# A pooling stage in which the 5/7 class reads its gathered source directly, and the next source gather waits for the first pooling pass

## The chip, the cores and the metric

One Trainium2 chip, one core of it. The time is the device time of the whole program in microseconds (us); the median of three runs before the change is 4460.77 us (4456.75 to 4460.80). The profile is of one further execution of the same program.

## What is computed

The input is 16 images of 512 channels, 64 x 64, float32. Two layers, each added to its own input:

```
x = x + relu(conv1x1(concat(gn(x), 25 neighbour correlations / norm)) + bias)      # layer 0
z = gn(x)                                                                          # layer 1
s = relu(w2 @ relu(w1 @ mean(z) + b1) + b2)          # one number per plane (image, channel)
q = clip(floor(s), 0, 5)
pools = maxpool_same(z, k) for k in (1, 3, 5, 7, 9, 11, 13)
x = x + (q + 1 - s) * pools[q] + (s - q) * pools[q + 1] + z
```

Each of the 8192 planes (16 images x 512 channels) thus needs two neighbouring pool sizes of its own: class q needs the windows 2q+1 and 2q+3. Class 2, the "third class" of this text, needs the 5 x 5 and the 7 x 7 maximum.

## The kernel before, in words

**First layer.** Up to about 2.6 ms the program goes through the images in chunks of eight rows. It writes the result y to DRAM (`y_planes`), and beside it `wide_planes`, in which each element is already the maximum of five neighbours in its row. Nothing of that is touched by the change.

**Sorting.** The classes are computed (`sort_planes`, L913), and the planes are sorted by class into tiles of 128 planes, one plane in a partition. A class fills whole tiles, so that NT is 72: in this data 67 tiles hold planes (classes 0 to 5 with 11, 11, 13, 11, 11 and 10 tiles, in this order: tiles 0 to 10, 11 to 21, 22 to 34, 35 to 45, 46 to 56, 57 to 66) and the last five are empty.

**Second layer, one tile t.** Five steps, each on its own engine, each engine with its own program of tiles. They meet by semaphores alone:

- POOL (GpSimd) gathers by indirect DMA: the records and the y planes of tile t into one of four buffers `bufs` (`gather`, L504), and the source planes of `wide_planes` into the single buffer `source` (`gather_source`, L521). For classes 0 and 1 the source gather has the indices of one plane only, all others being out of bounds, and the planes come from `bufs`; for class 2 and up it brings 128 planes of 16 KB.
- ACT (ScalarE) copies the source, or for classes 0 and 1 the y planes, into the single buffer `ypad` with four border columns left and right (`pad_plane`, L664: L673 the planes, L674 and L675 the borders).
- DVE (VectorE) takes maxima in two passes (`pools`, L1054; every operation is recorded as L1062). The first pass of class 2 goes over rows of `ypad` (`source_rows`, L1100), in 4 operations, and its second pass has 2 operations of 4096 elements. Classes 0 and 1 have 3 operations in the first pass. After the first pass `s_rows` is raised, after the second `s_pool`.
- PE (TensorE) sums the plane, the small and the large pool with diagonal matrices in eight PSUM banks (`mix`, L1383 and `mix_banks`, whose last product is L1406). It starts a bank when ACT has read it out for the tile before.
- ACT adds the constant and writes the banks back into `bufs` (`results`, L690; L695, eight times), then makes the diagonals of a later tile (L687). POOL scatters the tile to the output by indirect DMA (`scatter`, L535; L539).

**Order on the engines.** An engine takes its steps in the order in which they are written, so this order matters:

```
POOL  step t:  gather_source(t+1), wait for the write of t-2, gather(t+2), scatter(t-1)
ACT   step t:  pad_plane(t+1), results(t-1), diagonals(t+1)
DVE   tile t:  first pass, second pass
PE    tile t:  mix(t)
```

`scatter(t-1)` waits for `results(t-1)`; `gather_source(t+1)` is therefore behind `scatter(t-2)`. Before it issues, `gather_source(t)` waits until ACT has padded tile t-1 (`s_ypad`), since `source` may be overwritten then, copies the indices (L528) and issues (L531). `pad_plane(t)` waits until DVE has finished the first pass of t-1 (`s_rows`) and until the source has landed (`sourced`). DVE's tile t waits for its padding (`s_ypad`), for `mix(t-2)` (L1141 to L1143), and for its own last tile.

Of the kernel before, what the change touches and what calls it, by code (L numbers as in the profile page):

```python
# [15 lines left out]
P = 128  # L16
# [72 lines left out]
def build(nc, x, wt, wturn, bias, w1t, b1, w2t, b2, consts, out):  # L89
# [21 lines left out]
    with ctx:  # L111
# [108 lines left out]
        pos[0] = 0  # L220
        bufs = v(BUFS * PIX).rearrange("p (b n) -> p b n", b=BUFS)
        WP = W + 2 * PADC
        source = v(PIX)
        ypad_f = v((H + 2 * PADY) * WP)
        ypad = ypad_f.rearrange("p (h w) -> p h w", w=WP)
        hbuf_f = v((H + 2 * PADR) * W)
        hbuf = hbuf_f.rearrange("p (h w) -> p h w", w=W)
# [88 lines left out]

        GROUPED = 3 * QUADS * 16
        STATS_CHAIN = 7
        STATS_AT = 4

        def xs(ct, lo, n, par):
# [118 lines left out]
        def _(pool):  # L440
# [80 lines left out]
            def gather_source(t, b):  # L521

                if not (isinstance(t, int) and t == 0):
                    pool.wait_ge(s_ypad, t)
                    pool.sem_inc(s_issue, 1)
                    pool.wait_ge(sourced, t * 16)
                pool.sem_inc(s_issue, 1)
                pool.tensor_copy(src_idx[:, b:b + 1], src_ids[:, bass.ds(t, 1)]).then_inc(s_src, 1)  # L528
                pool.wait_ge(s_src, t + 1)
                pool.sem_inc(s_issue, 1)  # L530
                pool.indirect_dma_start(out=source, out_offset=None, in_=wide_dram[:, :],  # L531
                                        in_offset=bass.IndirectOffsetOnAxis(ap=src_idx[:, b:b + 1], axis=0),
                                        bounds_check=NPL - 1, oob_is_err=False).then_inc(sourced, 16)
# [43 lines left out]
        def _(act):  # L577
# [86 lines left out]
            def pad_plane(t, u):  # L664
                act.wait_ge(gathered[u], turns_done(t, u))
                if not (isinstance(t, int) and t == 0):
                    act.wait_ge(s_rows, t)
                act.wait_ge(sourced, (t + 1) * 16)
                with act.If(class_of(t) < NCLS):
                    at = act.value_load(src_at[0:1, bass.ds(t, 1)], min_val=0, max_val=BUFS)  # L670
                    rows_ = arena[:, bass.ds(at * PIX, PIX)].rearrange("p (h w) -> p h w", w=W)
                    inside = ypad[:, PADY:PADY + H, :]
                    act.activation(inside[:, :, PADC:PADC + W], rows_, ACT.Copy)  # L673
                    act.activation(inside[:, :, 0:PADC], rows_[:, :, 0:1].to_broadcast([P, H, PADC]), ACT.Copy)  # L674
                    act.activation(inside[:, :, PADC + W:WP], rows_[:, :, W - 1:W].to_broadcast([P, H, PADC]), ACT.Copy)\  # L675
                        .then_inc(s_ypad, 1)
                with act.Else():
                    if not (isinstance(t, int) and t == 0):
                        act.wait_ge(s_ypad, t)
                    act.sem_inc(s_ypad, 1)  # L680
# [55 lines left out]
        def _(dve):  # L736
# [176 lines left out]
            def sort_planes():  # L913
# [118 lines left out]
                link(dve.scalar_tensor_tensor(sel, tcls, float(NCLS), sel, ALU.is_lt, ALU.mult))  # L1032
                dve.tensor_scalar(not_first, ident[:, 0:1], -float(NPL), float(NPL), ALU.mult, ALU.add)
                link(dve.tensor_scalar(unsel, sel, -1.0, 1.0, ALU.mult, ALU.add))
                dve.tensor_copy(tmod, tmod_i)
                link(dve.tensor_scalar(unsel, unsel, not_first, None, ALU.mult))
                link(dve.tensor_scalar(src_f, tmod, -1.0, float(BUFS), ALU.mult, ALU.add))
                link(dve.tensor_tensor(src_f, src_f, sel, ALU.mult))
                link(dve.tensor_tensor(src_f, src_f, tmod, ALU.add))
                dve.tensor_copy(src_at, src_f)  # L1040
# [13 lines left out]
            def pools(t, s, k):  # L1054

                used = [0]

                def op(dst, a, b, wait=True, signal=s_own):

                    if wait and used[0]:  # L1060
                        dve.wait_ge(s_own, t * OWN + used[0])
                    ins = dve.tensor_tensor(dst, a, b, ALU.max)  # L1062
                    ins.then_inc(signal, 1)
                    if signal is s_own:
                        used[0] += 1

                def window(src, mid, dst, r, signal=s_own):

                    m, w = half_m, big[:, s, :]
                    op(mid(m, 0, 31 + r), src(1 - r, 31 + r), src(2 - r, 31 + r))  # L1070
                    core = m
                    if r in (2, 4):
                        op(mid(w, 0, 30 + r), mid(m, 0, 30 + r), mid(m, 1, 30 + r))
                        core = w
                    if r == 4:
                        op(mid(m, 0, 32), mid(w, 0, 32), mid(w, 2, 32))
                        core = m
                    if r in (3, 5):

                        op(mid(w, 0, 14 + (r + 1) // 2, 1), mid(m, 1, 14 + (r + 1) // 2, 2),  # L1080
                           mid(m, 2, 14 + (r + 1) // 2, 2))
                        if r == 5:
                            op(mid(w, 0, 16, 1), mid(w, 0, 16, 1), mid(w, 1, 16, 1))
                        op(mid(m, 0, 16, 2), mid(w, 0, 16, 1), mid(m, 0, 16, 2))
                        op(mid(m, 1, 16, 2), mid(w, 0, 16, 1), mid(m, r, 16, 2), wait=False)
                    op(dst(0), mid(core, 0, 32), src(-r, 32))
                    op(dst(1), mid(core, 0, 32), src(1 + r, 32), wait=False, signal=signal)

                planes = ypad[:, PADY:PADY + H, :]

                def cols(i, n):
                    return planes[:, :, PADC + i:PADC + i + 2 * n - 1:2]

                def cols_mid(a, i, n, step=1):
                    return a.rearrange("p (h w) -> p h w", w=36)[:, :, i:i + step * (n - 1) + 1:step]

                def rows(i, n):
                    return hbuf[:, PADR + i:PADR + i + 2 * n - 1:2, :]

                def source_rows(i, n):  # L1100
                    return ypad[:, PADY + i:PADY + i + 2 * n - 1:2, PADC:PADC + W]

                def rows_mid(a, i, n, step=1):
                    return a.rearrange("p (h w) -> p h w", w=W)[:, i:i + step * (n - 1) + 1:step, :]

                sm_, bg = small[:, s, :, :], big[:, s, :].rearrange("p (h w) -> p h w", w=W)
                inner = hbuf[:, PADR:PADR + H, :]
                small_rows = lambda e: sm_[:, e::2, 1:W + 1]

                def shifted(d):  # L1110
                    return planes[:, :, PADC + d:PADC + d + W]

                if k < 2:
                    window(cols, cols_mid, lambda e: inner[:, :, e::2], 1, signal=s_rows)
                elif k == 2:

                    window(source_rows, rows_mid, small_rows, k, signal=s_rows)
                elif k < 5:
                    op(inner, shifted(2 - k), shifted(k - 2), signal=s_rows)
                else:  # L1120
                    core = cols_mid(half_m, 0, 32)
                    op(core, cols(-2, 32), cols(3, 32))
                    op(inner[:, :, 0::2], core, cols(-3, 32))
                    op(inner[:, :, 1::2], core, cols(4, 32), wait=False, signal=s_rows)
                dve.wait_ge(s_rows, t + 1)
                if k == 0:

                    window(rows, rows_mid, lambda e: bg[:, e::2, :], 1, signal=s_pool)
                else:
                    if k != 2:  # L1130
                        window(rows, rows_mid, small_rows, k)
                    op(inner, sm_[:, :, 0:W], sm_[:, :, 2:W + 2])
                    op(bg, hbuf[:, PADR - 1:PADR - 1 + H, :], hbuf[:, PADR + 1:PADR + 1 + H, :], signal=s_pool)
                assert used[0] <= OWN
                dve.sem_inc(s_own, OWN - used[0])

            def tile(t, s):
                cls_t = dve.value_load(cls_i[0:1, bass.ds(t, 1)], min_val=0, max_val=NCLS)

                def waits():  # L1140
                    dve.wait_ge(s_ypad, t + 1)  # L1141
                    if not (isinstance(t, int) and t < 2):
                        dve.wait_ge(s_mix, (t - 1) * 8)  # L1143
                    if not (isinstance(t, int) and t == 0):
                        dve.wait_ge(s_pool, t)

                def branch(lo, hi):
                    if lo == hi:
                        waits()
                        if lo == NCLS:  # L1150
                            dve.sem_inc(s_own, OWN)
                            dve.sem_inc(s_rows, 1)
                            dve.sem_inc(s_pool, 1)
                        else:
                            pools(t, s, lo)
                        return
# [31 lines left out]
            for q in range(4):  # L1188
                dve.wait_ge(y_stored[q], 16 * B)
            for side in (slice(0, PADY), slice(PADY + H, H + 2 * PADY)):  # L1190
                dve.memset(ypad[:, side, :], LOWEST)
            for side in (slice(0, PADR), slice(PADR + H, H + 2 * PADR)):
                dve.memset(hbuf[:, side, :], LOWEST)
            dve.wait_ge(s_rec, 16)
# [242 lines left out]
```

## Time and profile before

| | |
|---|---|
| median of three runs | 4460.77 us |
| the profiled execution's own time | 4458.1 us |
| its span | 4456.4 us |
| PE busy | 3936.7 us, 88% |
| DVE busy | 3559.3 us, 80% |
| POOL busy | 2281.9 us, 51% |
| ACT busy | 1898.3 us, 43% |
| moved by DMA | 781.57 MB, 175 GB/s on average |

The span is the time from the first to the last instruction in the trace. Busy time of an engine is what its instructions took, not what they needed: an instruction that is held up while it runs counts as busy. The time of a whole engine says little here, because the program has a first layer, a sorting part and six stages of tiles with different limits. A row of the trace ends with the idle time of the engine just before it and with who ended it, in square brackets. On POOL and ACT that is often "issue", where the wait was for a DMA or lay in a branch, and the releaser isn't named.

### The profile page before, as it was taken

Reading aid. Unit: us, or ns where it says so; the run is one execution under the profiler, and the core shown is the slowest. Engines: PE = TensorE matmul, PEld = TensorE weight load, DVE = VectorE, ACT = ScalarE, POOL = GpSimd, SP = SyncE. Lnnn points to the kernel's source line nnn. Section 1 sums busy time; section 2 is a strip of 40 time slices with the busy share of each in tenths; the row PEclk is TensorE's granted clock in tenths of the full one; section 3 lists DMA queues with packets and bytes.
Section 4 is the critical chain, followed back from the end, with each engine's and each line's share of the span. In section 5 each row is a group of like instructions: output and inputs, shape, how many; then the busy total and the mean of one; then the engine's idle time right before and its main releaser. Section 6 shows DMA issues by size and latency. Waiting matters only on the chain. (4 is left out here: it accounts for less than half of the span.)

```text
span 4456.4 us, 76765 instructions
## 1 busy us (share of the span) xinstructions
PE 3936.7 (88%) x23656; PEld 2172.9 (49%) x23657; DVE 3559.3 (80%) x3528; ACT 1898.3 (43%) x2964; POOL 2281.9 (51%) x1793
## 2 busy tenths in 40 slices
PE   5999999999999999999999965789888888888885
PEld 3556555555555655656556642334333333333332
DVE  6887788787888788878878766689866799999993
ACT  3444444444444544444444513444333333333332
POOL 3555555555555555555555514355544444556442
PEclk9999999999999999999999977889998999999897
DMA  4444344544544444444443334444456566565551
GB/s 183 154 170 176 132 173 167 176 148 157 188 155 162 168 151 167 177 147 158 176 167 138 121 80 171 191 184 189 188 219 237 194 235 250 224 245 208 226 211 50
DMA packets 252266, 781.57 MB, mean 175 GB/s; under 512 B 98151, under 2 KB 98151, under 8 KB 229991
## 3 DMA queue, kind: packets, MB, share of 16 engines
q1 hardware_dynamic: 219600, 417.85, 26.8%
q0 software_dynamic: 32288, 358.95, 20.8%
q8 instruction: 206, 3.38, 0.3%
q14 instruction: 172, 1.40, 0.1%
HBM read 428.22 MB, written 409.08 MB: 188 GB/s over the span
## 5 line engine op out<-in xcount | busy, mean ns | idle before, releaser
L1062 DVE TENSOR_TENSOR arena<-arena 128x2048 f32<-128x2048 f32 (+5 forms) x539 | 1442.5, 2695 | 263.0 <-ACT arena L675 223.8
L1402 PE MATMUL psum<-arena 128*128 128x512 f32 x1072 | 606.7, 650 | 295.5 <-ACT arena L695 209.4
L1208 PE MATMUL psum<-arena 128*128 128x256 f16 (+1 forms) x6344 | 763.1, 276 | 47.2 <-DVE arena L808 34.4
L447 POOL TENSOR_TENSOR arena<-arena 128x512 f16<-128x512 f32 x512 | 721.5, 1417 | 146.5 <-ACT arena L597 140.6
L1231 PE MATMUL psum<-arena 128*128 128x512 f16 x2048 | 776.8, 379 | 0.0
L1233 PE MATMUL psum<-arena 128*128 128x512 f16 x2048 | 776.2, 379 | 0.0
L1232 PE MATMUL psum<-arena 128*128 128x512 f16 x2048 | 776.2, 379 | 0.0
L1208 PEld LDWEIGHTS psum<-arena 128*128 128x128 f16 x6344 | 610.9, 102 | 160.1 <-DVE arena L808 44.5
L673 ACT ACTIVATE arena<-arena 128x4096 f32 x67 | 242.5, 3619 | 1045.5 <-issue 1045.5
L456 POOL TENSOR_TENSOR arena<-arena 128x512 f32 (+1 forms) x512 | 635.1, 1273 | 10.7 <-ACT arena L611 6.7
L820 DVE BATCH_NORM_STATS2 bny<-arena 128x6 f32 (+1 forms) x512 | 355.6, 694 | 341.2 <-POOL arena L456 328.0
L1406 PE MATMUL psum<-arena 128*128 128x512 f32 x1072 | 579.2, 624 | 0.0
L611 ACT ACTIVATE arena<-psum,bias_sb 128x512 f32<-128x512 f32 x512 | 338.1, 686 | 541.8 <-POOL arena L456 339.8
L466 POOL CAST arena<-arena 128x128 f16<-128x128 f32 x128 | 37.3, 291 | 1006.1 <-DVE arena L852 1006.1
L1402 PEld LDWEIGHTS psum<-arena 128*128 128x128 f32 x1072 | 215.3, 207 | 591.5 <-issue 324.7
L1404 PE MATMUL psum<-arena 128*128 128x512 f32 x896 | 494.6, 635 | 0.0
L595 ACT ACTIVATE arena<-arena,gbias,grstd 128x512 f32 (+1 forms) x512 | 413.6, 808 | 48.9 <-POOL arena L447 46.0
L597 ACT ACTIVATE arena<-arena,gbias,grstd 128x512 f16 (+1 forms) x512 | 411.4, 803 | 0.0
L539 POOL DMA_INDIRECT out<-arena x67 | 120.0, 1791 | 551.7 <-issue 551.7
L1406 PEld LDWEIGHTS psum<-arena 128*128 128x128 f32 x1072 | 218.2, 204 | 288.1 <-issue 288.1
L808 DVE TENSOR_TENSOR arena<-psum,cst 128x256 f32<-128x256 f32 x496 | 287.4, 579 | 80.2 <-PE psum L1208 80.2
L695 ACT ACTIVATE arena<-psum,arena 128x512 f32<-128x512 f32 x536 | 319.5, 696 | 64.4 <-PE psum L1406 64.4
(161 smaller groups left out, 4328.5 us busy)
## 6 DMA issues: line engine op xcount, KB each, us to landing
arena<-in_x SPq DMA_DIRECT2D x64, 2048.0 KB, 13.3
wide_planes<-arena SPq DMA_DIRECT2D x128, 1024.0 KB, 5.3
y_planes<-arena SPq DMA_DIRECT2D x64, 2048.0 KB, 7.8
arena<-arena SPq DMA_DIRECT2D x1536, 8.0 KB, 1.8
arena<-wide_planes,arena POOLq DMA_INDIRECT x72
arena<-plane_records,arena POOLq DMA_INDIRECT x67
arena<-y_planes,arena POOLq DMA_INDIRECT x67
out<-arena POOLq DMA_INDIRECT x67, 7.9
```

The source lines that it names most:

```text
L447: pool.tensor_tensor(gl[:, ct, slot], g32[:, ct % 2, :], gh[:, ct, slot], ALU.subtract).then_inc(s_gl, 1)
L456: pool.tensor_tensor(y, y, relu[:, o % 2, :], ALU.add).then_inc(s_added, 1)
L595: act.activation(g32[:, ct % 2, :], piece, ACT.Identity, bias=gbias[:, ct:ct + 1], scale=grstd[:, ct:ct + 1])
L597: act.activation(gh[:, ct, (c % RING) * CW:(c % RING + 1) * CW], piece, ACT.Identity, bias=gbias[:, ct:ct + 1], scale=grstd[:, ct:ct + 1]) ...
L1062: ins = dve.tensor_tensor(dst, a, b, ALU.max)
L1208: return pe.matmul(dst, w, m, start=(k == 0), stop=(k == nk - 1))
L1231: pe.matmul(dst, h, gh[:, ct, slot], start=(ct == 0), stop=False)
L1232: pe.matmul(dst, h, gl[:, ct, slot], start=False, stop=False)
L1233: last = pe.matmul(dst, l, gh[:, ct, slot], start=False, stop=(ct == CT - 1))
L1402: pe.matmul(dst, diag[:, s, 0, :], bufs[:, u, b * CW:(b + 1) * CW], start=True, stop=False)
L1404: pe.matmul(dst, diag[:, s, 1, :], small[:, s, b * ROWS:(b + 1) * ROWS, 1:W + 1], start=False, stop=False)
L1406: pe.matmul(dst, diag[:, s, 2, :], big[:, s, b * CW:(b + 1) * CW], start=False, stop=True)\
```

## The change

The buffer `source` gets two rows above and two below it (`source_pad`), filled once with the lowest float; `ypad` loses its own. Class 2's first pass on DVE reads `source_pad` and waits for `sourced` instead of `s_ypad`. ACT's copy to `ypad` stays for all classes, class 2 among them. Since DVE may now be reading `source`, `gather_source(t)` waits for `s_rows` of tile t-1 beside `s_ypad`, for every class. The table that holds where each tile's planes come from is now in units of two rows (SRC_STEP).

```
-        source = v(PIX)
-        ypad_f = v((H + 2 * PADY) * WP)
+        source_pad = v((H + 2 * PADY) * W).rearrange("p (h w) -> p h w", w=W)
+        source = source_pad[:, PADY:PADY + H, :].rearrange("p h w -> p (h w)")
+        ypad_f = v(H * WP)
...
                 if not (isinstance(t, int) and t == 0):
                     pool.wait_ge(s_ypad, t)
+                    pool.sem_inc(s_issue, 1)
+                    pool.wait_ge(s_rows, t)
                     pool.sem_inc(s_issue, 1)
                     pool.wait_ge(sourced, t * 16)
...
-                    at = act.value_load(src_at[0:1, bass.ds(t, 1)], min_val=0, max_val=BUFS)
-                    rows_ = arena[:, bass.ds(at * PIX, PIX)].rearrange("p (h w) -> p h w", w=W)
-                    inside = ypad[:, PADY:PADY + H, :]
-                    act.activation(inside[:, :, PADC:PADC + W], rows_, ACT.Copy)
+                    at = act.value_load(src_at[0:1, bass.ds(t, 1)], min_val=0, max_val=SRC_AT)
+                    rows_ = arena[:, bass.ds(at * SRC_STEP, PIX)].rearrange("p (h w) -> p h w", w=W)
+                    act.activation(ypad[:, :, PADC:PADC + W], rows_, ACT.Copy)
...
-                dve.tensor_copy(tmod, tmod_i)
+                link(dve.tensor_copy(tmod, tmod_i))
                 link(dve.tensor_scalar(unsel, unsel, not_first, None, ALU.mult))
-                link(dve.tensor_scalar(src_f, tmod, -1.0, float(BUFS), ALU.mult, ALU.add))
+                link(dve.tensor_scalar(tmod, tmod, float(PIX // SRC_STEP), None, ALU.mult))
+                link(dve.tensor_scalar(src_f, tmod, -1.0, float(SRC_AT), ALU.mult, ALU.add))
...
                 def source_rows(i, n):
-                    return ypad[:, PADY + i:PADY + i + 2 * n - 1:2, PADC:PADC + W]
+                    return source_pad[:, PADY + i:PADY + i + 2 * n - 1:2, :]
...
-                def waits():
-                    dve.wait_ge(s_ypad, t + 1)
+                def waits(k):
+                    if k == 2:
+                        dve.wait_ge(sourced, (t + 1) * 16)
+                    else:
+                        dve.wait_ge(s_ypad, t + 1)
```

## Rows read from the trace of the kernel before

**Rows 1.** The page: the span.

```profile
span 4456.4 us, 76765 instructions
```

**Rows 2.** Busy us by stretch (PE, PEld, DVE, ACT, POOL), clock, DMA: classes 0, 1, 2, 5.

```profile
2700.00:2918.00 218.00, 158.79 (x320) 67.28 (x320) 149.67 (x66) 100.25 (x152) 89.59 (x75) 0.84 0.48 186
2918.00:3180.00 262.00, 237.18 (x512) 102.61 (x512) 247.09 (x89) 112.14 (x170) 149.53 (x77) 0.92 0.47 181
3180.00:3537.00 357.00, 297.36 (x624) 127.38 (x624) 233.65 (x78) 127.13 (x192) 172.66 (x91) 0.90 0.56 218
...
4109.00:4389.00 280.00, 228.93 (x480) 97.84 (x480) 275.65 (x120) 102.03 (x159) 109.79 (x72) 0.91 0.51 197
```

**Rows 3.** Waits, 3232 to 3537 us: who, for whom, total us, times, longest.

```profile
DVE arena L1062 <- ACT arena L675: 104.3, 11, 9.7
```

**Rows 4.** ACT's timeline, class 2: start us, us, what, count, idle before.

```profile
3255.68 3.62 ACT L673 ACTIVATE arena<-arena 128x4096 f32 x1 [17.77 <-issue]
...
3259.81 4.72 ACT L695 ACTIVATE arena<-psum,arena 128x512 f32<-128x512 f32 x8
...
3283.67 3.62 ACT L673 ACTIVATE arena<-arena 128x4096 f32 x1 [18.03 <-issue]
...
3532.89 3.62 ACT L673 ACTIVATE arena<-arena 128x4096 f32 x1 [17.64 <-issue]
```

**Rows 5.** POOL's timeline, class 2: scatter, index copy, source gather.

```profile
3266.18 1.87 POOL L539 DMA_INDIRECT out<-arena  x1 [11.55 <-issue]
3268.06 1.34 POOL L528 COPY arena<-arena 128x1 int32 x1
3270.31 4.57 POOL L531 DMA_INDIRECT arena<-wide_planes,arena  x1 [0.91 <-POOL arena L528]
```

**Rows 6.** DVE's timeline, class 2: tile 25.

```profile
3260.14 9.21 DVE L1062 TENSOR_TENSOR arena<-arena 128x2112 f32<-128x2112 f32 x4 [9.48 <-ACT arena L675]
3269.51 8.89 DVE L1062 TENSOR_TENSOR arena<-arena 128x4096 f32<-128x4096 f32 x2 [0.15 <-DVE arena L1062]
```

**Rows 7.** POOL's timeline, the first tiles.

```profile
2703.64 2.28 POOL L531 DMA_INDIRECT arena<-wide_planes,arena  x1 [0.90 <-POOL arena L528]
...
2715.03 2.35 POOL L531 DMA_INDIRECT arena<-wide_planes,arena  x1 [0.90 <-POOL arena L528]
...
2733.40 1.01 POOL L539 DMA_INDIRECT out<-arena  x1 [9.19 <-issue]
```

**Rows 8.** PE's timeline, class 2: first and last products of tile 24.

```profile
3260.53 2.08 PE L1402 MATMUL psum<-arena 128*128 128x512 f32 x2 [4.45 <-ACT arena L695]
...
3282.59 1.02 PE L1406 MATMUL psum<-arena 128*128 128x512 f32 x2
```

**Rows 9.** DVE's timeline, tiles 0 and 1.

```profile
2700.41 27.46 DVE L1062 TENSOR_TENSOR arena<-arena 128x2048 f32<-128x2048 f32 x12 [17.05 <-ACT arena L675]
```

**Rows 10.** ACT's timeline, padding of tiles 1, 2 and 3.

```profile
2709.42 3.62 ACT L673 ACTIVATE arena<-arena 128x4096 f32 x1 [8.07 <-issue]
...
2722.32 3.62 ACT L673 ACTIVATE arena<-arena 128x4096 f32 x1 [7.70 <-issue]
...
2742.57 3.62 ACT L673 ACTIVATE arena<-arena 128x4096 f32 x1 [9.65 <-issue]
```

**Rows 11.** POOL's timeline, class 1 to 2: source gathers 22, 23, scatter 20.

```profile
3162.47 2.19 POOL L531 DMA_INDIRECT arena<-wide_planes,arena  x1 [0.91 <-POOL arena L528]
...
3184.41 1.02 POOL L539 DMA_INDIRECT out<-arena  x1 [8.38 <-issue]
...
3187.68 2.19 POOL L531 DMA_INDIRECT arena<-wide_planes,arena  x1 [0.91 <-POOL arena L528]
```

**Rows 12.** DVE's timeline, class 1 to 2: from tile 21's second pass.

```profile
3163.88 34.08 DVE L1062 TENSOR_TENSOR arena<-arena 128x2048 f32<-128x2048 f32 x11 [0.16 <-DVE arena L1062]
```

**Rows 13.** DVE's timeline, class 5: tile 59's last operation, then tile 60.

```profile
4188.51 37.07 DVE L1062 TENSOR_TENSOR arena<-arena 128x4096 f32<-128x4096 f32 x15
```

**Rows 14.** ACT's timeline, class 5: padding of tile 61.

```profile
4207.59 3.62 ACT L673 ACTIVATE arena<-arena 128x4096 f32 x1 [15.90 <-issue]
```

More of the change, by code:

```diff
@@ L318, in build @@
         STATS_CHAIN = 7
+        SRC_STEP = PADY * W
+        SRC_AT = BUFS * PIX // SRC_STEP + 1
         STATS_AT = 4
@@ L669, in pad_plane @@
                 with act.If(class_of(t) < NCLS):
-                    at = act.value_load(src_at[0:1, bass.ds(t, 1)], min_val=0, max_val=BUFS)
-                    rows_ = arena[:, bass.ds(at * PIX, PIX)].rearrange("p (h w) -> p h w", w=W)
-                    inside = ypad[:, PADY:PADY + H, :]
-                    act.activation(inside[:, :, PADC:PADC + W], rows_, ACT.Copy)
-                    act.activation(inside[:, :, 0:PADC], rows_[:, :, 0:1].to_broadcast([P, H, PADC]), ACT.Copy)
-                    act.activation(inside[:, :, PADC + W:WP], rows_[:, :, W - 1:W].to_broadcast([P, H, PADC]), ACT.Copy)\
+                    at = act.value_load(src_at[0:1, bass.ds(t, 1)], min_val=0, max_val=SRC_AT)
+                    rows_ = arena[:, bass.ds(at * SRC_STEP, PIX)].rearrange("p (h w) -> p h w", w=W)
+                    act.activation(ypad[:, :, PADC:PADC + W], rows_, ACT.Copy)
+                    act.activation(ypad[:, :, 0:PADC], rows_[:, :, 0:1].to_broadcast([P, H, PADC]), ACT.Copy)
+                    act.activation(ypad[:, :, PADC + W:WP], rows_[:, :, W - 1:W].to_broadcast([P, H, PADC]), ACT.Copy)\
                         .then_inc(s_ypad, 1)
@@ L1087, in window @@
                     op(dst(1), mid(core, 0, 32), src(1 + r, 32), wait=False, signal=signal)
-                planes = ypad[:, PADY:PADY + H, :]
                 def cols(i, n):
-                    return planes[:, :, PADC + i:PADC + i + 2 * n - 1:2]
+                    return ypad[:, :, PADC + i:PADC + i + 2 * n - 1:2]
                 def cols_mid(a, i, n, step=1):
@@ L1110, in shifted @@
                 def shifted(d):
-                    return planes[:, :, PADC + d:PADC + d + W]
+                    return ypad[:, :, PADC + d:PADC + d + W]
                 if k < 2:
@@ L1148, in branch @@
                     if lo == hi:
-                        waits()
+                        waits(lo)
                         if lo == NCLS:
@@ L1190, in _ @@
             for side in (slice(0, PADY), slice(PADY + H, H + 2 * PADY)):
-                dve.memset(ypad[:, side, :], LOWEST)
+                dve.memset(source_pad[:, side, :], LOWEST)
             for side in (slice(0, PADR), slice(PADR + H, H + 2 * PADR)):
```

## The prediction

> **What bounds the kernel now.** I read the views in this order. The page gives the span, 4456.4 us [rows 1], and no more that helps: the change lies behind 2.7 ms. Busy time by stretch shows what each class is limited by. DVE is busy 276 of 280 us in class 5 and 247 of 262 in class 1, but only 150 of 218 in class 0 and 234 of 357 in class 2 [rows 2]. So in class 2, where the change is made, neither DVE nor PE (297 of 357) is full. The waits say that DVE stands 104.3 us there for ACT's padding, 9.5 us a tile [rows 3]. That looks like the thing to remove. The timelines tell otherwise. ACT pads tile 25 at 3255.68 for 4.25 us, writes the results of tile 23 from 3259.81 for 4.72, and pads tile 26 at 3283.67 [rows 4]. POOL begins the scatter of tile 23 at 3266.18, 1.65 us after those results; the index copy and the source gather of tile 26 stand behind it, and the gather's issue ends at 3274.88 [rows 5]; 8.8 us later the padding begins (8.4 to 8.8 in the tiles of class 2; I take 8.55). That is a closed ring: **pad, results, scatter, index copy, source gather, landing, pad**, 27.7 us a tile (from 3255.68 to 3532.89 in ten tiles [rows 4]). DVE is not a link of it. It only waits for it. Classes 0, 3 and 4 are on the same ring; classes 1 and 5 hang on DVE and PE.
>
> DVE does enter in another way. POOL's copy ends at 3269.40, as DVE's first pass does (3260.14 + 9.21 = 3269.35 [rows 6]), and the gather, 1.01 us for such an instruction when DVE rests [rows 7], takes 4.57 and ends 0.9 us after the first 4096 operation (3269.51 + 4.43 = 3273.94) [rows 5, 6]. So **a POOL instruction that falls into a DVE maximum ends when that maximum ends, a DMA one 0.93 us later**. The Trainium skill, "SBUF — State Buffer", section "Who interferes with whom", says that a VectorE instruction with two SBUF inputs contends with a GpSimd one that reads SBUF; by that the trace agrees.
>
> **The change, part by part.**
>
> *DVE's class 2 tiles start earlier, by up to 5.7 us.* They no longer wait for the 4.25 us of padding, nor for the at most 1.5 us in which ACT reads its two numbers. DVE is not in the ring, so the gain is 0 by itself. ACT still pads, so its link stays. What is late next is mix(t-2), which DVE waits for too: mix(24) goes from 3260.53 to 3283.61 [rows 8], when tile 26's padding begins [rows 4]. So DVE starts not 5.7 but some 4.5 us earlier.
>
> *Term 1, the added wait in class 0: +14.5 us.* In the ring of class 0 the source gather comes behind a scatter, and the first pass is over by then. In the first three tiles there is no scatter ahead yet. source(1) was released at 2700.4 by padding 0; now it waits for the end of DVE's third operation, 2700.41 + 3 x 2.29 = 2707.2 (12 operations in 27.46 [rows 9]). Copy, held until the fourth ends, 2709.6; 0.9 to the issue, 2710.5, held to 2711.9, end 2712.8, where it was 2705.92 [rows 7]. From there to the padding 3.5 us as before: 2716.3 for 2709.42 [rows 10], DVE's tile 1 at 2720.6. source(2): 2720.6 + 6.8 = 2727.4; by the same steps the issue ends at 2733.0 for 2717.38, and padding 2 begins at 2736.5 to 2737.9 for 2722.32 [rows 7, 10] (3.5 us as for tile 1, 4.9 as for tile 2), +14.2 to +15.6. The results of tile 0 stand behind it on ACT: 4.25 + 4.7 later, 2745.4 to 2746.8. Before, PE ended them at about 2731.8, and the scatter began at 2733.40; now at about 2747.7, +14.3. With that scatter the ring begins to turn, source(3) is behind it and waits for nothing else, padding 3 moves from 2742.57 [rows 10] by as much. The ring has no slack through class 0, and class 1 begins when it delivers: I take **+14.5**. Bounds: +12, if the landing is quicker; +17, if one more POOL instruction falls behind a maximum.
>
> In class 1 the gate puts off POOL by up to 5 us a tile. The source's issue ends 12.3 us after DVE's start (6.8 gate, 9.1 copy, 11.4 + 0.93); with 3.5 or 4.9 to the padding and 4.25 for it, 20 to 21.5 us, and DVE takes 22.5 a tile (247 us for eleven [rows 2]): hidden, with 1 to 3 us to spare. If that cover went, each of 11 tiles would cost what is over.
>
> *Term 2, into class 2: +7.* source(22) is the first full gather. DVE's tile 21 ends its first pass at 3163.7 [rows 12]; the copy is held to 3166.1, the issue to 3168.4 + 0.93 = 3169.3, for 3164.66 [rows 11]. Padding 22 is 3.9 us later, with it scatter(20): 3188.3 for 3184.41 [rows 11]. There DVE is in tile 22 (start 3179.7, unchanged: three operations to 3186.7, the fourth to 3188.9, 4096s to 3193.5 and 3197.9). Scatter ends at 3189.9, the copy at 3193.5, the gather at 3198.9 for 3189.87 [rows 11], and 8.55 us later is padding 23, 8.4 us later than before. Tile 24 by the same steps: the gap is 7.0. Bounds +3.7 (only the gate of tile 22 counts) and +9.
>
> *Term 3, class 2 itself: +8.* Let DVE start tile t at D. Its fifth operation is over at D + 13.8, its sixth at D + 18.25. The scatter, about 10.5 us after the padding begins, now falls into the fifth, so that it ends at D + 14.7; the copy falls into the sixth; the gather comes at D + 19.2, when DVE rests, and ends at D + 20.2; padding t+1 is 8.55 behind: **D + 28.8**. D itself is the end of mix(t-2), 27.9 us after padding t-1 began (3283.61 - 3255.68), plus 0.2. Two tiles thus take 28.8 + 28.1 = 56.9 us, for 2 x 27.7 = 55.4 now: +0.75 a tile, eleven tiles, +8. Bounds: DVE starts as soon as the source lands, 27.3 a tile, -4; mix ends later than I take it, +1.2 a tile, +13. I take the middle, since mix's end has a row.
>
> *No cost.* Classes 3 and 4: the first pass is one operation of 4.43 us, over before the scatter, and the ring has the same steps as now. Class 5: DVE starts tile 60 at 4188.51 + 4.43 = 4192.9 [rows 13]; gate +6.8, issue's end +11.8, padding at 20 to 21, done at 25, DVE's next tile at 28.0; before, padding 61 began at 4207.59 [rows 14], 14.7 after that start. Hidden behind DVE with 3 us over; without that cover it would be a us or two in ten tiles. Two more semaphore instructions on POOL a tile run while the scatter issues. One dependent step more in the sorting, well under 1 us. Copies from `source_pad` are of equal size.
>
> **Sum.** 14.5 + 7 + 8 = +29.5 on the profiled execution's 4458.1 gives 4487.6. The median of the runs is 2.7 above that execution, so I forecast **4490 us**.
>
> **The rivals.**
>
> *The gate alone counts (4475 to 4480).* Term 1 and 3.7 to 4 us at tile 22, and in class 2 the holds of POOL come out even, as at the lower bound of term 3. For it: only the order of some 2 us steps decides. Against: rows 5 and 6 show the hold in both kinds of POOL instruction.
>
> *POOL's DMA instructions are not held at all, only its copies (4465).* Then in class 2 the scatter is done inside the fifth operation, the copy ends with it at D + 13.8, the gather at D + 15.8, padding follows at D + 24.3. Two tiles take 52.4 us, 1.5 a tile less than now, -17: 4460.8 + 14.5 + 7 - 17 = 4465. Against: the gather's 4.57 us beside 1.01 [rows 5, 7].
> A remark in the same section of the Trainium skill's "SBUF — State Buffer" has it that two-input maxima did not stall a DMA's issue; this would be its outcome.
>
> *The late start is swallowed (4461 to 4466).* DVE idles 7 to 8 us a tile in class 0, and a ring that ran ahead at the start might have lost its lead anyway. Against: padding 1 to 3 are links of the ring, and nothing later in class 0 is ahead of it.
>
> *Faster: DVE is the link in class 2 after all (4401).* If what POOL waits for were released by DVE, the 5.7 us would come off each of 13 tiles, -74, and with term 1 that is 4461 - 74 + 14.5 = 4401. For it are rows 3. It decides from the point at which pool(t-1), not the banks, holds PE back. Against: PE's first product waits for L695, that is for a bank [rows 8].
>
> *Worse (over 4504).* Cover in class 1 or 5 fails, or class 3 loses a us a tile like class 2: 4501 to 4511.
>
> **How the numbers follow.** My forecast 0.63, gate alone 0.17, swallowed 0.08, DMAs not held 0.02, faster 0.05, worse 0.05. My forecast's own range is, with the terms' bounds not all at one end, 4477 to 4503. The range that leaves out about 2 in 10 takes in the gate alone: **4474 to 4504**. A measurement of this kernel can tell 0.2%, 8.9 us: faster by more than that 0.05, within it 0.10, slower 0.85.
>
> **What would show it.** In the new profile: padding 3 (L673, copy to `ypad`) some 14 us later than 2742.57, and the same 14 at the start of class 1; POOL's copy and gather of the first tiles ended behind the third maximum; in class 2 DVE ended by PE's last product or a DMA instead of ACT, the copy grown from 1.34 to 3 or more us and the gather's issue shrunk from 4.57 to about 1; paddings 28 to 29 us apart for 27.7; classes 3 to 5 as long as now. I am wrong if the paddings in class 2 are 27.7 or less apart, or if the first tiles keep their times.

## The result, and the profile after

| | before | after |
|---|---|---|
| median, 4 runs each | 4458.76 us (4455.32 to 4460.80) | 4488.01 us (4484.72 to 4488.70) |
| ratio after to before, 95% interval | | 1.0067 (1.0055 to 1.0079) |
| the profiled execution's own time | 4458.1 us | 4484.7 us |
| its span | 4456.4 us | 4483.0 us |

The change costs 29 us, 0.67%. The page's first lines, the span and the engines' busy time, do not say where:

```profile
span 4483.0 us, 76901 instructions
PE 3932.8 (88%) x23656; PEld 2171.5 (48%) x23657; DVE 3559.3 (79%) x3529; ACT 1895.7 (42%) x2964; POOL 2243.9 (50%) x1793
```

DVE does the same 3559.3 us of work. Busy time by stretch, classes 0, 1, 2 and 5, in the columns of [rows 2]:

```profile
2703.00:2935.00 232.00, 161.55 (x320) 68.17 (x320) 149.33 (x66) 99.95 (x151) 86.58 (x75) 0.83 0.45 174
2935.00:3188.00 253.00, 227.84 (x512) 98.20 (x512) 246.02 (x88) 106.17 (x164) 158.20 (x77) 0.97 0.46 183
3188.00:3560.00 372.00, 301.40 (x625) 128.80 (x624) 234.58 (x79) 129.91 (x196) 142.40 (x92) 0.89 0.54 213
4134.00:4415.00 281.00, 228.14 (x480) 97.63 (x480) 276.03 (x121) 101.27 (x160) 97.12 (x72) 0.90 0.50 196
```

Class 0 is 14 us longer (232 for 218), class 2 15 (372 for 357), and class 1 is 9 us **shorter** (253 for 262), at a granted clock of 0.97 for 0.92. The stages cut by the starts of DVE's tiles in the two traces, in us:

| | before | after | difference |
|---|---|---|---|
| DVE starts tile 0 at | 2700.4 | 2703.4 | +3.0 |
| tile 0 to 3 | 46.6 | 60.9 | +14.3 |
| 3 to 11, the rest of class 0 | 171.3 | 171.2 | -0.1 |
| 11 to 22, class 1 | 261.4 | 253.2 | -8.2 |
| 22 to 24 | 52.7 | 56.5 | +3.8 |
| 24 to 35, class 2 | 305.0 | 317.7 | +12.7 |
| 35 to 57, classes 3 and 4 | 571.5 | 571.5 | 0.0 |
| 57 to the end of 66, class 5 | 280.0 | 280.5 | +0.5 |
| from there to the end | 67.5 | 68.1 | +0.6 |

The sum is +26.6, the difference of the spans. Tile 0's start lay between 2698.1 and 2706.1 in the kernels run here and 0.4 to 3.6 us apart in two executions of one program, so its +3.0 is not put down to the change. The medians lie 29.3 us apart, 2.6 more than the two profiled executions (4484.7 - 4458.1): after's is 3.3 us above its profiled execution, before's 0.7. A fourth run of the kernel before, 4455.32, has moved its median from 4460.77 to 4458.76.

**The first tiles.** ACT's timeline, paddings 1 to 3 and the results of tile 0 (cf. [rows 10]):

```profile
2719.19 3.62 ACT L677 ACTIVATE arena<-arena 128x4096 f32 x1 [14.81 <-issue]
...
2739.18 3.62 ACT L677 ACTIVATE arena<-arena 128x4096 f32 x1 [14.79 <-issue]
...
2743.31 4.72 ACT L699 ACTIVATE arena<-psum,arena 128x512 f32<-128x512 f32 x8
...
2759.88 3.62 ACT L677 ACTIVATE arena<-arena 128x4096 f32 x1 [10.74 <-issue]
```

POOL's timeline there (L533 is the index copy, L536 the source gather, L544 the scatter; cf. [rows 7]):

```profile
2710.52 2.10 POOL L533 COPY arena<-arena 128x1 int32<-128x1 int32 x1 [14.21 <-DVE arena L1067]
2713.52 2.29 POOL L536 DMA_INDIRECT arena<-wide_planes,arena  x1 [0.89 <-POOL arena L533]
...
2749.62 1.74 POOL L544 DMA_INDIRECT out<-arena  x1 [8.61 <-issue]
2751.38 1.58 POOL L533 COPY arena<-arena 128x1 int32<-128x1 int32 x1
```

DVE's tile 0 starts at 2703.43. The copy is released by DVE and ends at 2712.6, 9.2 after that start, as its fourth operation does; the gather's issue ends at 2715.8, 12.4 after (the prediction had 12.4). From the start of tile 0, paddings 1, 2 and 3 lie 6.7, 13.8 and 14.3 us later than before.

**Class 2.** Who kept DVE waiting there (cf. [rows 3], 104.3 us for ACT):

```profile
DVE arena L1067 <- PE psum L1412: 113.3, 11, 11.7
```

ACT is gone from the list, and DVE waits 9 us longer for PE in its place. DVE, ACT and POOL around tiles 25 and 26:

```profile
3272.85 9.21 DVE L1067 TENSOR_TENSOR arena<-arena 128x2112 f32<-128x2112 f32 x4 [9.42 <-PE psum L1412]
3282.21 8.88 DVE L1067 TENSOR_TENSOR arena<-arena 128x4096 f32<-128x4096 f32 x2 [0.15 <-DVE arena L1067]
3302.83 2.36 DVE L1067 TENSOR_TENSOR arena<-arena 128x2112 f32<-128x2112 f32 x1 [11.73 <-PE psum L1412]
```

```profile
3274.05 3.62 ACT L677 ACTIVATE arena<-arena 128x4096 f32 x1 [19.41 <-issue]
...
3301.83 3.62 ACT L677 ACTIVATE arena<-arena 128x4096 f32 x1 [17.82 <-issue]
```

```profile
3284.55 2.98 POOL L544 DMA_INDIRECT out<-arena  x1 [14.28 <-issue]
3287.55 3.59 POOL L533 COPY arena<-arena 128x1 int32 x1
3292.05 1.06 POOL L536 DMA_INDIRECT arena<-wide_planes,arena  x1 [0.91 <-POOL arena L533]
```

The steps of term 3 stand here: the scatter ends 0.9 us after DVE's fifth operation (3287.53, 3286.64), the copy with its sixth (3291.1), the gather takes 1.06 us where it took 4.57 [rows 5], and it ends at D + 20.3 (D is where DVE's tile starts, 3272.85). The padding comes 8.7 us behind.

**The hold, counted.** In the trace of the kernel before, from tile 0 to the end of tile 66, 219 of POOL's indirect DMAs are issued while a maximum runs: 218 of them end 0.83 to 1.0 us after the end of that same maximum. Of 126 index copies that begin in a maximum, 115 end with it; the other 11 end some 0.1 us after it. POOL's memset in front of one of these copies, which reads nothing, isn't held (count, then shortest, median and longest in ns):

```profile
L506 POOL MEMSET arena<- x72: 102/102/126, 2682.1 to 4429.7; 128x4 f32 x72
L507 POOL COPY arena<-arena x72: 180/1712/4386, 2682.1 to 4429.7; 128x1 int32 x64, 128x1 int32<-128x1 int32 x8
```

### The profile page after: what moved, and what is told of

Read it like the earlier page. It is cut to its first block and busy times, and to the rows that moved or that the text cites. A ratio compares the mean times of both kernels' runs of the same rounds, so it can differ in the third digit from the quotient of the medians.

```text
span 4483.0 us, 76901 instructions
## 1 busy us (share of the span) xinstructions
PE 3932.8 (88%) x23656; PEld 2171.5 (48%) x23657; DVE 3559.3 (79%) x3529; ACT 1895.7 (42%) x2964; POOL 2243.9 (50%) x1793
## 5 line engine op out<-in xcount | busy, mean ns | idle before, releaser
L544 POOL DMA_INDIRECT out<-arena x67 | 146.2, 2181 | 595.9 <-issue 595.9
L699 ACT ACTIVATE arena<-psum,arena 128x512 f32<-128x512 f32 x536 | 317.1, 697 | 39.6 <-PE psum L1412 26.1
```

## The experiments

Eleven runs follow, of eight new kernels and three repeats, in three groups (e1 to e4, e5 to e8, e9 to e11); each ratio is to the kernel before as it ran in the same group, with medians of 4462.75, 4462.07 and 4458.70 us. e3, e4, e6, e7 and e11 were measured once each and have no interval. All stage times are of one profiled execution.

### Pulling the change apart: the gate alone

`e1_gate_only` keeps everything of the change but DVE's new wait:

```
-                    if k == 2:
-                        dve.wait_ge(sourced, (t + 1) * 16)
-                    else:
-                        dve.wait_ge(s_ypad, t + 1)
+                    dve.wait_ge(s_ypad, t + 1)
```

> The change with one part undone: DVE's class 2 tiles wait for the padding again, all else stays, the gate on the first pass in every class too. If class 2 is slower because DVE starts early and so lies across POOL's scatter and index copy (my theory), the paddings of class 2 are 27.7 us apart as before, against 28.5 in the change; the first tiles stay 14 us late; the step from class 1 to 2 costs 4 us; median about 4460 + 14 + 4, less the 8 us that class 1 gained, 4470. The rival, that the gate itself slows class 2, expects 28.5 us here too and about 4485.

Measured: 4535.67 us (4532.55 to 4540.13), ratio 1.0161 (1.0143 to 1.0179), far above what every theory had. `e11_gate_only_again` is the same program, measured once:

> The change with DVE waiting for the padding in class 2, once more, one look. If class 1 has two patterns between which an execution falls by the clock's phase, its eleven tiles take either 253 or 261 to 264 us here (264 the first time); if the program decides, 264 again. Class 2 again 32.3 us a tile: the gate opens at the end of the first pass, just when the first 4096 operation begins, and holds copy and gather one operation each longer.

Measured: 4542.19; class 1 takes 264.3 us, for 264.2 in e1. In both, class 2 takes 32.3 us a tile (tiles 24 to 35: 354.8 and 354.7 us, for 305.0). POOL and DVE around tile 25 of the first:

```profile
3302.14 1.86 POOL L544 DMA_INDIRECT out<-arena  x1 [14.97 <-issue]
3305.76 4.17 POOL L533 COPY arena<-arena 128x1 int32 x1 [1.76 <-DVE arena L1067]
3310.84 4.44 POOL L536 DMA_INDIRECT arena<-wide_planes,arena  x1 [0.91 <-DMA out<-arena]
```

```profile
3296.10 9.21 DVE L1067 TENSOR_TENSOR arena<-arena 128x2112 f32<-128x2112 f32 x4 [14.01 <-ACT arena L679]
3305.47 8.89 DVE L1067 TENSOR_TENSOR arena<-arena 128x4096 f32<-128x4096 f32 x2 [0.15 <-DVE arena L1067]
```

The first pass ends at 3305.31. Before, the copy had slipped in 1.3 us ahead of that end and was over with it, and only the gather was held, by the fifth operation [rows 5, 6]. Now the gate opens at that end, 0.16 us before the fifth operation starts; that one holds the copy to 3309.9, and the sixth holds the gather to 3315.3. The gather ends 23.6 us after the padding's start (3291.64) where it was 19.2, and a tile takes **4.5 us more, one whole maximum**, for a wait that by itself is over 1.8 us after the scatter. So in class 2 (tiles 22 to 35) the gate costs 62 us (12.4 + 49.8), and the early start of DVE gives back 46 of them (8.6 + 37.1). What that start would be worth without the gate, nothing by the prediction, no run shows. "The gate costs little and DVE's start nothing", from which I had built my expectation, was wrong twice.

### The gate in class 2 only, and both kernels again

`e2_gate_class2_only` lets POOL wait for `s_rows` only where tile t-1 is of class 2:

```
+                    last = class_of(t - 1)
+                    with pool.If(last < 3):
+                        with pool.If(last < 2):
+                            pool.sem_inc(s_issue, 1)
+                        with pool.Else():
+                            pool.wait_ge(s_rows, t)
+                            pool.sem_inc(s_issue, 1)
+                    with pool.Else():
+                        pool.sem_inc(s_issue, 1)
                     pool.wait_ge(s_ypad, t)
                     pool.sem_inc(s_issue, 1)
-                    pool.wait_ge(s_rows, t)
-                    pool.sem_inc(s_issue, 1)
```

> The change, but POOL waits for the first pass only when the tile before is of class 2 (which is all that needs it). My theory: padding 3 at its old distance from the stage's start (the 14 us of the first tiles gone), class 2 at 28.5 us a tile as in the change. On class 1, where the change gained 8 us that I had not foreseen: if the gate's delays spread PE's work and so keep its clock up, class 1 is here as long as before (about 262 us for its tiles) and the median about 4475; if the gain came by the chance of the clock's phase at the stage's entry, class 1 may be of either length, and the median 4467 to 4475.

Measured: 4474.42 (4468.73 to 4485.01), ratio 1.0029 (1.0014 to 1.0043). Paddings 0 to 3 in ACT's timeline (L684 in this kernel) are back at the old distances; padding 1 is 9.1 us after DVE's start of tile 0, for 9.0 in the kernel before and 15.8 in the change:

```profile
2697.12 3.62 ACT L684 ACTIVATE arena<-arena 128x4096 f32 x1 [64.26 <-issue]
2710.50 3.62 ACT L684 ACTIVATE arena<-arena 128x4096 f32 x1 [8.19 <-issue]
2723.29 3.62 ACT L684 ACTIVATE arena<-arena 128x4096 f32 x1 [7.58 <-issue]
2743.89 3.62 ACT L684 ACTIVATE arena<-arena 128x4096 f32 x1 [10.12 <-issue]
```

Tile 0 to 3 takes 47.0 us, so term 1 is the gate. Class 2 is 56.5 + 317.7, as in the change. Class 1 takes 253.4 in the profiled execution (4469.52), the change's short time, with no gate in it.

`e3_after_again` and `e4_before_again` are the two kernels once more, measured once each:

> The change once more, one look. If the spacing by the gate makes class 1 shorter, it is 8 us shorter here too, with TensorE's clock at 2.4 GHz through most of it; if that was chance, it may be as before.

> The kernel before once more, one look. If its class 1 is a stable pattern, every second tile of class 1 again waits 2.3 us for PE and the granted clock falls to 1.2 GHz once in two tiles; if it was chance, some tiles have no such wait.

Measured: 4486.29 and 4457.85, class 1 253.3 and 261.6 us. In e4 DVE again waits five times, 2.3 us each, and the clock falls once in two tiles. So before, the change and the gate alone (e1, e11) each have the same class 1 in both of their profiles. That makes an accident of one execution unlikely and doesn't exclude it: class 1 isn't known for the runs without a profile, and they spread over more than its 8 us, from 4468.73 to 4485.01 in e2 and from 4446.54 to 4470.58 in the kernel before in that group.

### The index copy taken out of the ring

The copy L528 needs nothing that it waits for; it can be made a step earlier, in `gather`, behind the other index copy. `e5_before_copy_ahead` does so in the kernel before, `e6_after_copy_ahead` in the changed one:

```
                 pool.tensor_copy(idx[:, b:b + 1], ids_i[:, bass.ds(t, 1)]).then_inc(s_idx, 1)
+                pool.tensor_copy(src_idx[:, b:b + 1], src_ids[:, bass.ds(t, 1)]).then_inc(s_src, 1)
...
-                pool.tensor_copy(src_idx[:, b:b + 1], src_ids[:, bass.ds(t, 1)]).then_inc(s_src, 1)
                 pool.wait_ge(s_src, t + 1)
```

> The kernel before, with one instruction moved: POOL copies the indices of the source gather with those of the plane gather, two tiles ahead, not between scatter and source gather. My theory (a POOL instruction that falls into a DVE maximum is held until it ends): in class 2 the source gather then comes before the first 4096 operation and is held only by the fourth of the first pass, so that it ends 4.5 us earlier in each tile's ring; class 2 falls from 27.7 to 23.5 us a tile, class 0 by 1 or 2 us a tile, classes 3 and 4 by no more than DVE's wait of 0.9 to 1.8 us; median about 4390. The rival, that POOL's instructions merely take long, expects the copy's own 1.3 us a tile off and no more: class 2 26.4, median about 4430.

> The same move in the changed kernel. By the hold theory the gather is now held by DVE's sixth operation in class 2 as the copy was, and only 1 us a tile is gained there: 27.5 us for 28.9; class 0 as in the run before it; about 4460. The rival (the copy's own time, 3.5 us a tile in class 2) expects 25.4 us a tile there and 4440.

Measured: e5 4424.58 (4422.96 to 4425.30), ratio 0.9915 (0.9898 to 0.9931); e6 4457.77, a single run. e5 around a tile of class 2:

```profile
3234.53 1.88 POOL L539 DMA_INDIRECT out<-arena  x1 [9.39 <-issue]
3236.71 1.90 POOL L531 DMA_INDIRECT arena<-wide_planes,arena  x1 [0.30 <-issue]
```

```profile
3228.49 18.24 DVE L1062 TENSOR_TENSOR arena<-arena 128x2112 f32<-128x2112 f32 x6 [5.57 <-ACT arena L675]
```

The gather falls into the fourth maximum, which ends at 3237.7, and is over 0.9 us later, at 3238.6; 14.6 us after the padding began for 19.2 before. The hold theory gave just that for the issue, where the rival had 1.3 us. But a tile takes 25.7 us, not 4.5 less than 27.7: the source lands 9.7 us after the issue's end (3248.3), where it took 7.1 in e1 and in e9. So the total missed the theory's 4390 by 35 us, and stands nearer to the rival's 4430; it is the rows that decide between the two. The DMA view of 3225 to 3260 us (the last number is the time from issue to landing):

```profile
out<-arena POOLq DMA_INDIRECT x1, 8.9
arena<-wide_planes,arena POOLq DMA_INDIRECT x1, 11.6
```

The gather now follows the scatter by 2.2 us, and both move 2 MB. Of the 4.6 us won at the issue, 2.0 are left at the tile. In class 0, where the source gather brings one plane only, it lands 0.2 to 0.7 us behind the scatter (2783.80 and 2783.61 us in one tile), so that there the earlier issue brings nothing: class 0 is as long as before. The Trainium skill, "DMA: Bandwidth & Descriptors", section "Two DMAs through the same engine are not ordered", says that descriptors within one queue of one DMA engine start in order but are pipelined. The landings here fit that; no row shows the descriptors' own order.

In e6, class 2 takes 27.2 us a tile, within 0.3 of what was expected, where the rival had 25.4. Its total of 4457.77 for 4460 is in part luck: class 1 is back at 261.7 us (+8.5), against tiles 0 to 3 with 56.5 us for 60.9 and class 4 with 6.5 us less.

### Is ACT's dead copy a link?

In class 2 nobody reads `ypad` any more. `e7_no_padding_class2` skips that copy in the changed kernel and only counts `s_ypad` up; it was measured once:

```
+                cls_t = class_of(t)
+                with act.If(cls_t < 3):
+                    with act.If(cls_t < 2):
+                        copy_plane(t)
+                    with act.Else():
+                        if not (isinstance(t, int) and t == 0):
+                            act.wait_ge(s_ypad, t)
+                        act.sem_inc(s_ypad, 1)
```

> The change, but ACT leaves out the copy to ypad in class 2, which nothing reads any more. If the padding is a link of the ring, as I hold, the results come 4.25 us earlier and class 2 shortens, by what the holds leave of it: the scatter falls behind the fourth operation, copy and gather behind the fifth and sixth, some 26.5 us a tile for 28.9, 4460. If the padding is off the path that sets the pace (rival), class 2 stays at 28.9 and the time at 4487.

Measured: 4461.98; tiles 24 to 35 in 298.0 us, 27.1 a tile, or 26.5 without the last step into class 3 (32.4 us), and tiles 22 to 24 in 53.6. DVE's tile 26:

```profile
3294.56 7.01 DVE L1079 TENSOR_TENSOR arena<-arena 128x2112 f32<-128x2112 f32 x3 [8.34 <-DMA arena<-wide_planes,arena]
```

It starts when the source lands. The 4.25 us of a copy that nobody reads stood ahead of the results on ACT and so in the ring. Without it tiles 22 to 35 take 22.7 us less than in the change (351.5 for 374.2), and the one run is about as long as the kernel before in its group (4462.07).

### PE's products before the pools

PE waits for pool(t) before it starts, though its first product of each bank needs only the plane. `e9_products_ahead` is the changed kernel with these eight products issued first, and the wait behind them:

```
-                pe.wait_ge(s_pool, t + 1)
...
+                    pe.matmul(psum[:, b, :], diag[:, s, 0, :], bufs[:, u, b * CW:(b + 1) * CW], start=True, stop=False)
+                pe.wait_ge(s_pool, t + 1)
+                for b in range(8):
                     dst = psum[:, b, :]
-                    pe.matmul(dst, diag[:, s, 0, :], bufs[:, u, b * CW:(b + 1) * CW], start=True, stop=False)
```

> The change, and PE does the eight products that need no pool (plane times diagonal) before it waits for the pools, the other two of each bank after. mix then ends some 6 us sooner after a pool. My theory: in class 1 DVE never waits for mix(t-2) and its eleven tiles take 250 us, whatever the clock does; in class 2 DVE starts when the source lands, the pair of tiles 56.9 us long becomes 2 x 27.5, 14 us less in the stage; the last tile ends 6 us sooner. Median about 4465. The rival, that class 2's 28.9 us do not hang on mix(t-2), expects class 2 unchanged and 4479; that the clock sets class 1 in another way than by DVE's wait, 253 to 262 us there.

Measured: 4468.50 (4463.44 to 4471.31), ratio to before 1.0021 (1.0012 to 1.0031), 19.5 us below the changed kernel's median, which is of another group of runs. Class 1 takes 250.3 us and DVE waits for no mix there. Class 2 was to lose 14 us and took 317.8, as without the edit, which is what the rival expected. Its waits in class 2:

```profile
DVE arena L1067 <- PE psum L1414: 113.7, 11, 11.9
```

and PE's eight early products of tile 24 (L1407):

```profile
3271.58 10.20 PE L1407 MATMUL psum<-arena 128*128 128x512 f32 x16 [6.27 <-ACT arena L699]
```

PE starts when ACT frees the banks (L699), not when the pool comes, so all 24 products still lie behind that release and mix(24) ends where it did: 3295.5, and DVE's tile 26 starts at 3295.6, 2.6 us after its source landed. This supports term 3's reading that D is mix(t-2)'s end: the rival was right in the number and wrong in the cause. The spans of the two profiled executions (4465.3, 4483.0) differ by 17.7 us: 3.7 in tile 0's start, 2.9 in class 1, and 10.6 behind DVE's last operation (57.5 us for 68.1), where eight products of 0.86 us of the last mix are done before, and where in the changed kernel PE rested 4.3 us ahead of the last mix and its first three products took 1.9 to 2.1 us each for 1.02.

### The combinations

`e8_all_three`: the gate in class 2 only, no copy to `ypad` in class 2, the index copy ahead. `e10_all_and_products`: the same and PE's products first.

> The change with the gate in class 2 only, no padding in class 2, and the indices copied ahead. Start of the stage as before (14 us less than the change), class 2 limited by the sum of PE's eight banks and DVE, 23.4 us a tile, class 0 and 4 1 us a tile less: about 4385, faster than both kernels by 1.6% or more. If PE's clock or the DMAs set the pace of class 2 instead, 25 us a tile and 4405.

> The best version so far (gate in class 2 only, no padding there, indices copied ahead) with PE's eight products ahead of the pools. Class 1 250 us for 262, class 2 22.5 us a tile for 24.3, the end 6 us sooner: about 4376. If class 2 is by now limited by POOL's holds alone, 24 us a tile and 4393.

Measured: e8 4412.11 (4411.10 to 4414.34), ratio 0.9887 (0.9871 to 0.9904), class 2 24.3 us a tile; e10 **4391.93** (4386.24 to 4393.53), ratio 0.9850 (0.9834 to 0.9867), class 2 23.9 a tile, class 1 250.3. e10 missed 22.5 us a tile and 4376 and came out at the alternative, 24 us and 4393; that POOL's holds are what limits it isn't shown, since DVE still waits mostly for PE. DVE's waits of e10 in class 2:

```profile
DVE arena L1086 <- PE psum L1433: 51.6, 9, 7.1
DVE arena L1086 <- DMA arena<-wide_planes,arena: 10.9, 3, 3.7
```

e10 is 1.5% quicker than the kernel before. With the held copy out of the ring, reading the source directly and leaving out the dead copy together do pay: e8 is 12 us below e5 (4412.11, 4424.58), which has the copy ahead alone, and its tiles 24 to 35 take 267.3 us for 282.8. e8 missed its expectation by 27 us: 10 in class 2 (24.3 a tile for 23.4), class 0 gained nothing from the copy ahead (its source lands behind the scatter's transfer), and class 1 fell back to 261.9.

## Why the prediction was right, and where it was not

**Term 1, +14.5: measured +14.3**, and gone where the gate is gone (e2). The ring that "has no slack through class 0" passed it on: tiles 3 to 11 take 171.2 us for 171.3, and the rival in which the late start is swallowed is refuted.

**Terms 2 and 3, +7 and +8, together +15: measured +16.5** between tiles 22 and 35. Cut by the paddings, as the prediction has them, both stand alone: against DVE's start of tile 22, paddings 22, 23 and 24 lie 4.2, 8.7 and 7.7 us later than before (forecast 3.9, 8.4 and 7.0), and the eleven tiles from padding 24 to 35 take 313.7 us for 304.9, +8.8. The table's 3.8 and 12.7 are the same sum cut by DVE's starts, which class 2 moves ahead and class 3, waiting for the padding again, moves back. The padding is 28.5 us apart (3244.67 to 3558.4 in eleven tiles) for the 28.45 forecast, and two tiles take 57.2 (3244.67 to 3301.83) for 56.9. The rival in which POOL's DMA instructions are not held, 4465, is refuted: the scatter takes 2.98 us and ends 0.9 after the maximum it fell into. So is the rival in which DVE is the link: its wait changed hands at once, and the time rose. One reading behind the hold was wrong and did no harm: the 1.01 us of [rows 7] isn't an instruction beside a resting DVE. That scatter begins 0.1 us before the end of the first maximum of tile 2 (2731.23 to 2733.52) and ends 0.9 us after it, as held ones do. The figure at rest is the change's 1.06 us.

**What the prediction did not have: class 1, -8.2.** I wrote that the gate is hidden there and the class keeps its length. The gate is hidden; the length is not fixed. Before, DVE waits for mix there:

```profile
DVE arena L1062 <- PE psum L1406: 11.3, 5, 2.3
```

Five times 2.3 us. PE, before, around one of these (clock below, by windows), and after at the same tile:

```profile
3080.81 1.02 PE L1406 MATMUL psum<-arena 128*128 128x512 f32 x2
3085.39 2.07 PE L1402 MATMUL psum<-arena 128*128 128x512 f32 x2 [3.56 <-issue]
3087.26 1.91 PE L1404 MATMUL psum<-arena 128*128 128x512 f32 x2
```

```profile
3075.01 1.12 PE L1408 MATMUL psum<-arena 128*128 128x512 f32 x2 [1.89 <-ACT arena L699]
```

Busy time and granted clock (before's row, then after's) for 3084 to 3092 us:

```profile
3084.00:3092.00 8.00, 6.61 (x9) 2.86 (x10) 7.79 (x5) 0.00 (x0) 6.68 (x3) 0.57 0.88 371
```

```profile
3084.00:3092.00 8.00, 8.00 (x20) 3.57 (x19) 7.95 (x3) 2.19 (x1) 5.93 (x4) 1.00 0.20 82
```

Before, from mix(13) on, PE rests 3.6 us ahead of every second mix, the granted clock is then at 1.2 GHz (0.5) for 6.8 us, and three products take 1.9 to 2.1 us each for 1.02. That mix ends 2.3 us after DVE could start, DVE waits, the next mix follows without a rest, and then PE rests 3.6 us again: once in 47.8 us, four times, behind a first rest of 7.3 us. After, PE rests 3.6 us ahead of mix(13) and then 1.9 us ahead of each of five mixes, the clock stays at 2.4 GHz from 2964 to 3121, and DVE waits for mix only twice, 3.0 us in all. In no profile does one pattern turn into the other within the class. The class took 261 to 262 us in the first (before twice, e5, e6, e8, and e1 and e11 with 264, 3.0 of which are DVE's wait for the padding of tile 22) and 253 to 254 in the second (after twice, e2, e7). The runs show that neither the gate (e1 has it and takes 264, e2 has none there and takes 253) nor class 2's part of the change (e6 has it and takes 261.7) decides it alone, and that it came out alike in both profiles of three programs; the clock falls or does not fall at tile 13 behind a rest of the same 3.6 us. What tips it there stays **open**; DVE's wait for mix(11) ahead of it is 2.0 to 2.4 us in the first pattern and 1.0 to 1.95 in the second, which goes with it and may not be the cause. An untested rival is chance, by the moment at which the clock changes against the tiles: the fall around DVE's start of tile 11 begins 0.9 to 1.7 us ahead of that start in the seven profiles of the first pattern, and in the four of the second 2.0 or 0.2 us ahead of it, or 1.2 and 1.5 behind it. What removes it is shown: with PE's products ahead, e10 has 250.3 us where e8 has 261.9.

**The sum.** +29.5 was forecast on the profiled time, and +26.6 measured: +14.3 + 16.5 - 8.2 in class 1, + 3.0 at tile 0's start, and +1.0 over the rest. The median, 4488.01 for 4490, is nearer than the sum deserves, and that is luck: against class 1's -8.2, which was left out, stand the +3.0 and +1.0, 1.3 us more in the three terms, and an after whose median happens to lie 3.3 us above its profiled execution.

**The rival "the gate alone counts" was badly priced.** It put the change at 4475 to 4480 and DVE's early start at nothing. The gate alone, e1, has 4536. The step that failed is "in class 2 the holds of POOL come out even": before, the copy has a lead of 1.3 us on the next maximum, and the gate takes it away; the rival's price left that out. That the full change came out at the forecast is due to D's shift: DVE is further on when POOL comes, so that the scatter and the copy fall into its last two maxima and the gather comes when DVE rests.

**My expectation for e9** failed for the reason that the prediction itself had named against DVE as the link: in class 2 PE's first product waits for a bank, not for a pool [rows 8].

## What to carry to other kernels

Find the ring of waits and price an edit by its links; a long wait of an engine (104 us of DVE here) may hang on the ring without being in it, and work left in the ring that nobody reads (ACT's copy) undoes the gain of a shortcut around it. A new wait costs not what it lasts but what it makes the waiting engine miss: here 1.8 us of waiting put POOL's copy behind one more maximum, 4.5 us a tile. Keep small POOL instructions out of a ring that DVE's two-input operations run beside, and issue work that needs no late input ahead of the wait for it.

## What the runs showed of the hardware

- **POOL is held to the end of a running maximum**, in every kernel here: the copy (0.18 us when DVE rests, 3.6 to 4.2 under a 4096 operation) ends with it, an indirect DMA's issue (1.0 us at rest, up to 5.2) 0.9 us after, while a memset (0.10 us) is not held. The Trainium skill, "SBUF — State Buffer", "Who interferes with whom", has the contention of a two-input VectorE instruction with GpSimd's reads, and the copy agrees with it; its remark that such operations did not stall a DMA's issue does not hold for these indirect ones (4.44 us in e1 for 1.06 in the change).
- **A 2 MB gather issued 2.2 us behind a 2 MB scatter lands 2.6 us later after its issue** (9.7 us in e5 for 7.1 in e1 and e9), so that 4.6 us won at the issue were 2.0 a tile at the landing.
- **A rest of 3.6 us ahead of a mix, with the fall of the clock to 1.2 GHz behind it, can come back once in two tiles through a whole stage.** That the one keeps up the other is read from the rows; what the runs show is that it is gone where DVE's wait is gone (e9, e10). It costs 0.7 us a tile in class 1 (8.2 in eleven), where neither engine's busy share in the page (88% and 80%) shows it.
